# Softmax rows shifted inside four exponentials on ScalarE, in place of one subtraction on VectorE

## The chip, the cores and the metric

The kernel runs on one core of one Trainium2 chip. The metric is device microseconds (us) of one execution: the median of three runs is 2493.81 us (2492.76 to 2499.24). The engines are TensorE (PE, with its weight loads as PEld), VectorE (DVE), ScalarE (ACT), GpSimd (POOL) and SyncE (SP), which only starts transfers. Each engine works through its own list of instructions in order, and the lists meet in semaphores.

## The reference, cut to what matters

The program is one transformer layer over 32 sequences of 64 tokens, width 1024, in float32. The part that the change touches is the softmax of the attention (32 query heads, 8 key heads, head width 128):

```python
x = x + attn(einsum(x, cond_weights[condition]))       # q, k: RMS-normed by head
scores = einsum("bkgqd,bksd->bkgqs", q, k) / sqrt(128)
bias = where(rel > 0, -1e30, slopes * rel)             # ALiBi, causal, rel = key - query
attn = softmax(scores + bias, axis=-1)
out = (attn @ v) @ Wo.T
x = x + ffn(cond2(x))                                  # two linear layers with low-rank parts
```

## The kernel before, in words

The 2048 tokens go in four blocks of 512, each of four tiles of 128 tokens. Of each block the kernel works through units: keys and values of two key heads (`kv`), queries of one key head's four heads (`q`, eight of them), the output projection of a pair of key heads (`o`, four), and the two halves of the feed-forward layer (`f`). Every float32 operand is split into a high and a low part of the type fp32r, and a product is three matmuls (line 927). The high part is a copy on ScalarE (line 1122), the low part a subtraction on VectorE (line 1372). Of a chunk of weights both parts go into `ring`. The output projection takes seven products of half-size blocks instead of eight; its left factors are sums of quarters (`quads`), split into `lefts`. In block 0 the right factors are also summed on VectorE (`sums`). The projection is the same in both kernels.

The order of all work is written by one planner. A `q` step is one unit and one tile: four chunks of six matmuls of 512 columns, with a clock tick of the planner after each chunk (a quarter). What follows on the other engines is put in by delays in quarters (the table `AT`): squares and the mean (ACT, DVE), the power -0.5 (`rstd`, POOL), the scaling of the queries (`scale`, DVE line 1499, writes `qn`), their transposes (PE line 1076), their split (`qt_hi`, `qt_lo`), the scores (PE lines 1092 and 1093), the softmax, the transposes of the probabilities (PE line 1100), their split and the product with the values (PE line 1111), whose result ScalarE copies to `quads`. Work that falls between these by its delay, the split of a weight chunk above all, stands between them in the lists of the engines. There are 128 `q` steps in the program (8 units x 4 tiles x 4 blocks), and the softmax of step k runs beside the matmuls of step k+1.

The softmax of a step has 128 partitions x 256 columns, which are four row groups of 64 keys. Its instructions are `alibied` and `biased` (VectorE, line 1375: the two parts of the scores in PSUM and the ALiBi table are added into `score`), `peak` (line 1535: maximum of each row group), `shifted` (line 1541: the maximum subtracted, in place), `exp` (ScalarE, line 1270), `total`, `inverse` and `prob` (VectorE, lines 1546, 1551, 1556: sum, reciprocal, product). The planner adds the first four as one group at 5.5 quarters, `exp` at 6.3, the last three at 6.4 and the transposes of `prob` at 7.9.

## Time and profile before

| What | Value |
| --- | --- |
| Runs, median (lowest, highest) | 2493.81 us (2492.76, 2499.24) |
| Profiled execution, its own time | 2496.57 us |
| Its span, first to last instruction | 2494.8 us |
| Mean granted clock of TensorE | 0.987 of full speed |
| Share of the span busy: PE, DVE, ACT | 96%, 71%, 50% |

The profiled execution took 1.8 us more than its span, and 2.76 us more than the median of the runs. A busy time is a sum over one engine; it does not say that an engine sets the time. The chain that ended last is followed back from the last instruction, at each step to what released it. Where it passes through an instruction with a piece of 0.04 us, the next instruction on the same engine started before that one had ended, and only the part before that start is put down to it; what follows as "issue" belongs to the same stretch of the engine's list.

### The profile page before, as it was taken

The numbers are of one execution on the slowest core, as the hardware profiler recorded it, in microseconds if no ns is written. First come the engines' busy times: TensorE is split into PE (matmuls) and PEld (weight loads), VectorE is DVE, ScalarE is ACT, GpSimd is POOL, SyncE is SP. The second block draws the span as 40 slices with busy tenths as digits, with TensorE's granted clock in tenths as the row PEclk, the third lists the DMA queues.
The fourth block names the chain that finished last, engine by engine and source line by source line (L and its number), as shares of the span: only waits on it lengthen the run. The fifth ranks groups of instructions, "written<-read, shape, count | busy, mean of one in ns | idle before, by whom it ended". The sixth has DMA issues, their size and how long they took to land.

```text
span 2494.8 us, 32612 instructions
## 1 busy us (share of the span) xinstructions
PE 2407.1 (96%) x11676; PEld 1984.4 (80%) x11676; DVE 1777.3 (71%) x2894; ACT 1242.0 (50%) x2881; POOL 244.9 (10%) x272
## 2 busy tenths in 40 slices
PE   7999999999899999999899999999989999999988
PEld 5877778878788888888778888888868888888867
DVE  5547879796836878787854777777864686868772
ACT  3234646464624555555533555555633564646550
POOL 0101000000011101010011101010110101010110
PEclk8999999999999999999999999999999999999999
DMA  5355454543432242424233141424243242424240
GB/s 206 117 215 206 167 187 153 202 145 109 152 112 100 80 144 81 143 81 143 102 130 143 68 152 68 152 68 152 76 146 135 68 144 76 150 70 152 69 169 34
DMA packets 88435, 316.12 MB, mean 127 GB/s; under 512 B 12716, under 2 KB 13228, under 8 KB 87124
## 3 DMA queue, kind: packets, MB, share of 16 engines
q1 hardware_dynamic: 70292, 247.14, 28.9%
q10 hardware_dynamic: 10944, 37.54, 4.0%
q0 software_dynamic: 7040, 29.36, 3.2%
q8 instruction: 95, 1.56, 0.2%
q14 instruction: 64, 0.52, 0.1%
HBM read 282.54 MB, written 31.46 MB: 126 GB/s over the span
## 4 chain that ended last, share of the span: by engine, by line
PE 85%; DVE 10%; issue 3%; DMA 1%; ACT 1%; ACTq 0%; POOL 0%; POOLq 0%; DVEq 0%
PE main L927 72%; DVE ring L1372 3%; PE qt_bank L1076 3%; PE s_bank L1092 2%; PE pv_bank L1111 2%; PE s_bank L1093 2%; DVE score L1375 2%; PE pt_bank L1100 1%; DVE qn L1499 1%; PE pt_bank L927 1%; PE s_bank L927 1%; PE qt_bank L927 1%; DVE peak L1535 1%; DMA sums<-in_wo 1%; DVE pt_lo L1562 0%
## 5 line engine op out<-in xcount | busy, mean ns | idle before, releaser
L927 PE MATMUL main<-ring,act_hi 128*128 128x512 f32 x3584 | 1150.9, 402 | 0.0
L927 PEld LDWEIGHTS main<-ring,act_hi 128*128 128x128 f32 x3584 | 643.2, 189 | 111.5
L927 PE MATMUL main<-ring,act_lo 128*128 128x512 f32 x1792 | 702.9, 392 | 0.0
L927 PE MATMUL main<-ring,lefts 128*128 128x512 f32 x2688 | 636.8, 395 | 24.0 <-issue 23.9
L1372 DVE TENSOR_TENSOR ring<-raw,ring 128x1024 fp32r<-128x1024 f32 x448 | 556.9, 1244 | 80.0 <-ACT ring L1122 78.5
L927 PEld LDWEIGHTS main<-ring,lefts 128*128 128x128 f32 x2688 | 507.6, 190 | 131.9 <-issue 27.1
L1122 ACT ACTIVATE ring<-raw 128x1024 fp32r<-128x1024 f32 x448 | 473.0, 1057 | 239.4 <-PE main L927 234.4
L927 PEld LDWEIGHTS main<-ring,act_lo 128*128 128x128 f32 x1792 | 337.4, 188 | 74.8
L1695 POOL TENSOR_TENSOR rstd<-mean,half 128x4 f32<-128x4 f32 (+1 forms) x192 | 174.7, 910 | 1694.6 <-DVE mean L1482 1694.6
L1244 ACT ACTIVATE sq<-main 128x128 f32<-128x128 f32 x640 | 168.8, 277 | 66.1 <-PE main L927 63.7
L1375 DVE TENSOR_TENSOR acc<-main,acc 128x512 f32<-128x512 f32 x164 | 112.4, 686 | 98.2 <-PE main L927 98.1
L1270 ACT ACTIVATE prob<-score 128x256 f32<-128x256 f32 x128 | 53.5, 418 | 230.6 <-DVE score L1541 230.6
L1562 DVE TENSOR_TENSOR pt_lo<-pt_bank,pt_hi 64x256 fp32r<-64x256 f32 x256 | 107.9, 421 | 75.0 <-ACT pt_hi L1279 73.3
L1372 DVE TENSOR_TENSOR lefts<-quads,lefts 128x1024 fp32r<-128x1024 f32 x112 | 136.7, 1221 | 26.8 <-ACT lefts L1122 24.5
L1279 ACT ACTIVATE pt_hi<-pt_bank 64x256 fp32r<-64x256 f32 x256 | 97.1, 379 | 115.9 <-PE pt_bank L1100 111.3
L1122 ACT ACTIVATE qt_hi<-qt_bank 128x512 fp32r<-128x512 f32 x128 | 76.7, 599 | 129.8 <-PE qt_bank L1076 129.4
L1499 DVE TENSOR_TENSOR qn<-main,rstd 128x512 f32<-128x512 f32 (+1 forms) x192 | 114.6, 597 | 33.7 <-POOL rstd L1695 33.7
L1372 DVE TENSOR_TENSOR qt_lo<-qt_bank,qt_hi 128x512 fp32r<-128x512 f32 x128 | 88.2, 689 | 67.6 <-ACT qt_hi L1122 66.2
L1244 ACT ACTIVATION_READ_ACCUMULATOR sq<-main 128x1 f32 x640 | 132.6, 207 | 0.0
L1122 ACT ACTIVATE lefts<-quads 128x1024 fp32r<-128x1024 f32 x112 | 118.5, 1058 | 27.6 <-PE main L927 20.2
L1092 PE MATMUL s_bank<-k_t,qt_hi 128*128 128x128 f32 x512 | 114.7, 285 | 7.4 <-issue 7.4
L1076 PEld LDWEIGHTS qt_bank<-ident,qn 128*128 128x128 f32 x640 | 76.6, 141 | 53.1 <-DVE qn L1499 27.3
(142 smaller groups left out, 2445.1 us busy)
## 6 DMA issues: line engine op xcount, KB each, us to landing
raw<-in_wq SPq DMA_DIRECT2D x128, 512.0 KB, 4.2
raw<-t_scratch SPq DMA_DIRECT2D x128, 512.0 KB, 3.2
raw<-in_wo SPq DMA_DIRECT2D x96, 512.0 KB, 3.2
raw<-in_wkv SPq DMA_DIRECT2D x64, 512.0 KB, 3.4
sums<-in_wo ACTq DMA_DIRECT2D x32, 512.0 KB, 6.7
t_scratch<-sums ACTq DMA_DIRECT2D x32, 512.0 KB, 3.7
raw<-f_scratch SPq DMA_DIRECT2D x32, 512.0 KB, 4.4
acc<-in_x POOLq DMA_DIRECT2D x16, 512.0 KB, 3.6
```

Of the source, the lines that this page charges most:

```text
L927: mm = eng.matmul(bank, a, b, start=start and n == 0 and m == 0, stop=stop and n == len(terms) - 1 and m == 2, skip_group_check=further)
L1076: mm = eng.transpose(qt_bank[:, tile(h)], norm_tile(k)[:, tile(h)], ident[:, :])
L1092: eng.matmul(s_bank[:, a:a + 2 * SEQ], lh, keys, start=True, stop=False)
L1122: eng.activation(dst, src, ACT.Copy).then_inc(done[stage], 1)
L1244: act = eng.activation(sq[:, tile(h)], norm_bank(k)[:, tile(h)], ACT.Square, accum_out=ssum[:, h:h + 1])
L1270: eng.activation(prob[:, :], score[:, :], ACT.Exp).then_inc(done["exp"], 1)
L1279: act = eng.activation(pt_hi[rows_of(b), b, :], pt_bank[rows_of(b), 0:256], ACT.Copy)
L1372: eng.tensor_tensor(dst, src, f32(upper), ALU.subtract).then_inc(done[stage], 1)
L1375: eng.tensor_tensor(dst, a, b, ALU.add).then_inc(done[stage], 1)
L1499: eng.tensor_tensor(heads_of(norm_tile(k)[:, cols], heads), heads_of(norm_bank(k)[:, cols], heads), along(rstd[:, 0:heads], heads), ALU.mu ...
L1562: rest = eng.tensor_tensor(pt_lo[rows_of(b), b, :], pt_bank[rows_of(b), 0:256], f32(pt_hi[rows_of(b), b, :]), ALU.subtract)
L1695: eng.tensor_tensor(rstd[:, 0:heads], mean[:, 0:heads], half[:, 0:heads], ALU.pow).then_inc(done[stage], 1)
```

## The change: minimum of the negated scores as the bias of four exponentials

The scores are now kept negated: the table `alibi` is negated on the host, `alibied` is table minus the first part of the scores, `biased` subtracts the second part. The maximum becomes a minimum of the negated rows. `shifted` is gone. The exponential takes -1 times the negated score plus the minimum of its row group. That minimum is a column of 128 values and differs from row group to row group, so the one instruction over 256 columns becomes four over 64 columns. The last of the four raises the semaphore that `total` waits for; the first waits for `peak`.

```diff
             self.queries_left = "score", (k,)
 
         def softmax():
-            for stage in ("alibied", "biased", "peak", "shifted"):
+            for stage in ("alibied", "biased", "peak"):
                 self.add(stage, k)
...
                 elif stage == "exp":
                     k, = key
-                    w.wait_ge("shifted", k)
+                    w.wait_ge("peak", k)
                     if order.number["prob_t", key] > 1:
                         w.wait_ge("prob_t", order.stages_of["prob_t"][order.number["prob_t", key] - 2][0])
                     else:
                         w.wait_ge("ones")
-                    eng.activation(prob[:, :], score[:, :], ACT.Exp).then_inc(done["exp"], 1)
+                    for r in range(4):
+                        cols = slice(r * SEQ, (r + 1) * SEQ)
+                        act = eng.activation(prob[:, cols], score[:, cols], ACT.Exp, bias=peak[:, r:r + 1], scale=-1.0)
+                    act.then_inc(done["exp"], 1)
...
                         table = alibi[:, 2 * g:2 * g + 2, :].rearrange("p h (o n) -> p h o n", o=1)
-                        add(rows, parts[:, :, :, 0, :], table.broadcast_to([P, 2, BPT, SEQ]), stage)
+                        eng.tensor_tensor(rows, table.broadcast_to([P, 2, BPT, SEQ]), parts[:, :, :, 0, :],
+                                          ALU.subtract).then_inc(done[stage], 1)
                     else:
                         w.wait_ge("alibied", k)
-                        add(rows, parts[:, :, :, 1, :], rows, stage)
+                        eng.tensor_tensor(rows, rows, parts[:, :, :, 1, :], ALU.subtract).then_inc(done[stage], 1)
                 elif stage == "peak":
                     k, = key
                     w.wait_ge("biased", k)
                     eng.tensor_reduce(peak[:, :], score[:, :].rearrange("p (r n) -> p r n", n=SEQ), AXIS.X,
-                                      ALU.max).then_inc(done[stage], 1)
-                elif stage == "shifted":
-                    k, = key
-                    w.wait_ge("peak", k)
-                    by_row = score[:, :].rearrange("p (r n) -> p r n", n=SEQ)
-                    eng.tensor_tensor(by_row, by_row, peak[:, :].rearrange("p (r o) -> p r o", o=1).broadcast_to([P, 4, SEQ]),
-                                      ALU.subtract).then_inc(done[stage], 1)
+                                      ALU.min).then_inc(done[stage], 1)
...
-    return table.reshape(HEADS // 2, 2, SEQ, SEQ).transpose(1, 2, 0, 3).reshape(P, HEADS // 2, SEQ)
+    return -table.reshape(HEADS // 2, 2, SEQ, SEQ).transpose(1, 2, 0, 3).reshape(P, HEADS // 2, SEQ)
```

On VectorE, in the third `q` step of block 1 (`ring` is the split of a weight chunk, `qn` the scaling of the next step's queries), there stands before:

```order
L1375 TENSOR_TENSOR score<-s_bank,alibi 128x256 [waits s_score]
L1375 TENSOR_TENSOR score<-s_bank,score 128x256 [waits s_alibied]
L1535 TENSOR_REDUCE peak<-score 128x4 [waits s_biased]
L1541 TENSOR_TENSOR score<-score,peak 128x256 [waits s_peak]
L1372 TENSOR_TENSOR ring<-raw_65,ring 128x1024 [waits s_w_hi]
L1499 TENSOR_TENSOR qn_72<-main,rstd 128x512 [waits s_query_t,s_rstd]
L1546 TENSOR_REDUCE total<-prob 128x4 [waits s_exp]
```

and now:

```order
L1532 TENSOR_TENSOR score<-alibi,s_bank 128x256 [waits s_score]
L1536 TENSOR_TENSOR score<-score,s_bank 128x256 [waits s_alibied]
L1540 TENSOR_REDUCE peak<-score 128x4 [waits s_biased]
L1375 TENSOR_TENSOR ring<-raw_65,ring 128x1024 [waits s_w_hi]
L1502 TENSOR_TENSOR qn_72<-main,rstd 128x512 [waits s_query_t,s_rstd]
L1545 TENSOR_REDUCE total<-prob 128x4 [waits s_exp]
```

The row of line 1541 is gone and nothing else has moved: the split of the weights, the scaling and `total` follow in the same order, one place earlier.

On ScalarE, at the same step (`quads` is the copy of the previous step's attention output, `ring` the high part of a weight chunk, `qt_hi` that of the transposed queries), there stands before:

```order
L1122 ACTIVATE ring<-raw_65 128x1024 [waits s_raw1]
L1270 ACTIVATE prob<-score 128x256 [waits s_shifted]
L1122 ACTIVATE quads<-pv_bank 128x2x4x64 [waits s_pv]
L1122 ACTIVATE ring<-raw_66 128x1024 [waits s_raw2]
L1122 ACTIVATE qt_hi<-qt_bank 128x4x2x64 [waits s_score,s_query_t]
```

and now:

```order
L1122 ACTIVATE ring<-raw_65 128x1024 [waits s_raw1]
L1272 ACTIVATE prob<-score,peak 128x64 [waits s_peak]
L1272 ACTIVATE prob<-score,peak 128x64 x3
L1122 ACTIVATE quads<-pv_bank 128x2x4x64 [waits s_pv]
L1122 ACTIVATE ring<-raw_66 128x1024 [waits s_raw2]
L1122 ACTIVATE qt_hi<-qt_bank 128x4x2x64 [waits s_score,s_query_t]
```

One exponential has become four at the same place, the first with a wait for `peak` in place of `shifted`; the copies behind them keep their order.

## Rows read from the trace of the kernel before

**Rows 1.** The page: busy us (share of the span) and instructions.

```profile
PE 2407.1 (96%) x11676; PEld 1984.4 (80%) x11676; DVE 1777.3 (71%) x2894; ACT 1242.0 (50%) x2881; POOL 244.9 (10%) x272
```

**Rows 2.** Waits: who waited <- for what: us in total, times, longest us.

```profile
ACT prob L1270 <- DVE score L1541: 230.6, 127, 5.6
...
PEld qt_bank L1076 <- DVE qn L1499: 27.3, 41, 3.6
...
PE main L927 <- issue: 23.9, 6, 5.8
...
PEld pt_bank L1100 <- DVE prob L1556: 2.9, 7, 0.5
```

**Rows 3.** Two stretches: length, busy PE PEld DVE ACT POOL, PEclk, DMA.

```profile
780.00:1204.00 424.00, 423.17 (x2067) 349.74 (x2067) 324.50 (x566) 235.67 (x593) 39.32 (x43) 1.00 0.31 107
1204.00:1245.00 41.00, 34.44 (x161) 27.70 (x160) 37.38 (x57) 25.93 (x52) 2.02 (x2) 0.94 0.37 128
```

**Rows 4.** Timeline of a step: start us, us, engine, line.

```profile
811.78 1.01 POOL L1695 TENSOR_TENSOR rstd<-mean,half 128x4 f32<-128x4 f32 x1 [6.76 <-DVE mean L1482]
...
812.67 0.42 DVE L1535 TENSOR_REDUCE peak<-score 128x4 f32<-128x256 f32 x1
...
813.12 0.42 DVE L1541 TENSOR_TENSOR score<-score,peak 128x256 f32<-128x256 f32 x1
...
813.46 1.22 DVE L1372 TENSOR_TENSOR ring<-raw,ring 128x1024 fp32r<-128x1024 f32 x1
...
813.58 0.42 ACT L1270 ACTIVATE prob<-score 128x256 f32<-128x256 f32 x1 [1.12 <-DVE score L1541]
813.90 0.59 ACT L1122 ACTIVATE quads<-pv_bank 128x512 f32<-128x512 f32 x1
...
814.60 0.68 DVE L1499 TENSOR_TENSOR qn<-main,rstd 128x512 f32<-128x512 f32 x1
...
814.38 0.61 PE L927 MATMUL main<-ring,act_hi 128*128 128x512 f32 x2
814.83 0.39 PE L927 MATMUL main<-ring,act_lo 128*128 128x512 f32 x1
815.34 0.66 PE L1076 MATMUL qt_bank<-ident,qn 128*128 128x128 f32 x4
```

**Rows 5.** Chain that ended last: start us, us, what.

```profile
202.24 0.04 DVE score L1541
...
1208.41 0.04 DVE score L1541
...
1216.82 0.04 DVE score L1541
...
1225.65 0.42 DVE score L1541
...
2382.93 0.42 DVE score L1541
```

**Rows 6.** Groups by line and shape: count, busy us, mean ns, idle before.

```profile
L1541 DVE TENSOR_TENSOR score<-score,peak 128x256 f32<-128x256 f32 x128 | 54.4, 425 | 4.4
...
L1270 ACT ACTIVATE prob<-score 128x256 f32<-128x256 f32 x128 | 53.5, 418 | 230.6 <-DVE score L1541 230.6
```

**Rows 7.** Line 1407, PSUM as its second operand: ns min/median/max.

```profile
L1407 DVE TENSOR_TENSOR qn<-kept,main x2: 673/676/680, 21.5 to 23.5; 40x512 f32<-40x512 f32 x2
```

**Rows 8.** ScalarE instructions back to back.

```profile
9.81 0.70 ACT L1152 ACTIVATE pt_hi<-prob 128x256 fp32r<-128x256 f32 x2
...
11.04 0.29 ACT L1122 ACTIVATE qt_hi<-prob 128x128 fp32r<-128x128 f32 x1
...
1212.61 0.77 ACT L1279 ACTIVATE pt_hi<-pt_bank 64x256 fp32r<-64x256 f32 x2 [1.02 <-PE pt_bank L1100]
```

**Rows 9.** Timeline of a step: probabilities done, loaded by PE.

```profile
1047.69 0.42 DVE L1556 TENSOR_TENSOR prob<-prob,inv 128x256 f32<-128x256 f32 x1
...
1048.94 0.37 PEld L1100 LDWEIGHTS pt_bank<-ident,prob 128*128 128x128 f32 x2
```

## The prediction

> **What bounds the kernel now.** I read the busy shares first, then the waits, two stretches by their busy times, the chain that ended last, and at last single steps in order of time. TensorE is busy 96% of the span, VectorE 71%, ScalarE 50% [rows 1]. Between 780 and 1204 us TensorE's records fill 423.17 of 424 us and VectorE's 324.50; from 1204 to 1245 us TensorE's fill 34.44 of 41 and VectorE's 37.38 [rows 3]. So TensorE bounds the kernel in most places, and at the end of a block VectorE does. What VectorE costs elsewhere must be looked for in short waits: the transposes of the queries wait for the scaling `qn` 41 times, 27.3 us in all, and at the end of a block the projection waits up to 5.8 us [rows 2]. ScalarE has waited for the subtraction 127 times before its exponential, 230.6 us in all [rows 2]; that is cover in front of the exponential, and shows that ScalarE is the early one there.
>
> **The subtraction goes.** Each of the 128 takes 425 ns, 54.4 us in all [rows 6]. In the step at 813 us the maximum starts at 812.67, the subtraction at 813.12, the split of a weight chunk at 813.46 [rows 4]. The last started 0.34 us after the instruction before it; behind the maximum it would start at 813.01. So 0.45 us of VectorE's list goes per step, 57.6 us over 128. It is worth time only where the subtraction is on the path. It stands in the chain that ended last 44 times, from 202.24 to 2382.93 us [rows 5]. I sort the 44 by what follows.
>
> *Short waits, 26 times.* Behind the subtraction stand a split of 1.22 us and the scaling, and TensorE waits for the latter. In the step shown, two products take from 814.38 to 814.83, thus 0.225 us each. The transposes start 0.51 us after the product at 814.83, which is 0.28 us late [rows 4]. With the scaling 0.45 us earlier (from 814.60 to 814.15) nothing is left of that. Nor is another releaser just behind: GpSimd's `rstd` ended at 812.79 [rows 4]. 26 x 0.28 = 7.3 us.
>
> *Block 0, six times.* There the sums of the right factors stand in the same list, and VectorE works without a pause from the subtraction to the instruction that TensorE waits for. Each gives its whole 0.45 us: 2.7 us.
>
> *Ends of blocks, three in each of four.* In block 1 these are at 1208.41, 1216.82 and 1225.65 us [rows 5]. VectorE is busy 37.38 of those 41 us [rows 3], and the projection behind them waits up to 5.8 us [rows 2]. A shorter list moves the end of that wait by all that it is shortened: 12 x 0.45 = 5.4 us.
>
> The other 84 subtractions are not in the chain. TensorE's products hide them, and I count them at nothing. If that cover were gone they would be worth 84 x 0.45 = 38 us.
>
> **Four exponentials for one.** The present one takes 418 ns [rows 6]. The trace has no exponential of 64 columns and none whose bias is a column. Nearest from below: copies from SBUF of 256 columns, two in 0.70 us, so thus 0.40 us each and 0.30 apart, an overlap of 0.10; one of 128 columns takes 0.29 us [rows 8]. On this line 64 columns take 0.24 us and start 0.14 apart: four take 3 x 0.14 + 0.24 = 0.66 us. From above: the two copies of 256 columns and 64 partitions from PSUM take 0.77 us and don't overlap, 0.385 each [rows 8]; four such take 1.54 us. I take 0.66, since the copies from SBUF are the nearer rows, and keep 1.54 for the range. The exponentials start 0.45 us earlier than now (behind the maximum), so they end 0.45 - (0.66 - 0.42) = 0.21 us earlier than now, or 0.67 us later by the upper bound. What is queued behind them is the copy of the attention output (at 813.90 in the step shown) [rows 4] and the high part of the next weight chunk; what waits for them is `total`. In the step at 1046 us `total` follows the exponential directly, the normalised rows are done at 1047.69 + 0.42 = 1048.11 and TensorE loads them at 1048.94 [rows 9]: 0.83 us to spare, more than 0.67. TensorE waited for `prob` only 7 times, 2.9 us in all [rows 2]. So in most steps even the upper bound costs nothing. At the ends of blocks it does: there ScalarE's copies feed VectorE's list, and 0.67 us later would eat the 0.45 us of each subtraction. By the upper bound the 12 give nothing, or lose 12 x 0.22 = 2.6 us more if all of it shows.
>
> The Trainium skill (ScalarE: Activation LUTs, What ACT_TABLE_LOAD costs) has a rule that speaks against this change: an ACTIVATE costs a fixed 186 ns and 0.833 ns a column, a bias that is a column adds about 93 ns, and neighbours overlap by about 93 ns. The present trace agrees on the fixed part and the overlap (0.40 us for 256 columns, 0.30 apart) and is silent on the bias. By that page four take 3 x 0.24 + 0.33 = 1.05 us; the sum would then lose about 0.1 us at each of the twelve places, and the time would come out some 1.2 us higher.
>
> **Edits at nothing.** Adding becomes subtracting and maximum becomes minimum on the same shapes. The PSUM operand becomes the second one; a 512-column instruction of that kind takes 676 ns [rows 7], one with PSUM first 0.68 us [rows 4]. The bounds are -0.01 and +0.01 us, 256 times on VectorE, of which 88 in the chain: under 1 us either way. The negated table is made on the host; its transfer is the same. No transfer is moved.
>
> **The sum.** 7.3 + 2.7 + 5.4 = 15.4 us. The profiled execution took 2496.57 us and would take 2481.2; the median of the runs is 2.76 us lower, so I predict 2493.81 - 15.4 = 2478.4 us, 0.6% less.
>
> **The rivals.**
> 1. *The short waits come back or were never the bound (no change).* The chain credits VectorE wherever it released TensorE last, even if by a hair, and the weight split before the scaling needs a high part from ScalarE, which now works longer. If the 26 short waits stay and the ends of blocks give nothing, 2.7 us are left: 2491 us. For it: in [rows 3] TensorE's records fill the long stretch but for 0.83 us, so there is little to see. Against it: the 0.51 us between two starts in [rows 4] is a gap in the starts themselves.
> 2. *ScalarE becomes the late one (slower).* The mechanism is one: the exponentials end so late that `prob` reaches the transposes late in ordinary steps. The place is line 1100, the point is 0.83 + 0.45 + 0.42 = 1.70 us for the four, 0.425 each without overlap [rows 9]. For it: an exponential takes 0.418 now, and reading a bias column is unseen. Against it: 256 columns become 64. At 0.5 us each the four take 2.0, 0.3 us beyond the point; if half of the 128 steps have no more slack than the one shown, 64 x 0.3 = 19 us are added, the ends of blocks give nothing, and it ends at 2493.8 - 10.0 + 19 = 2503 us.
> 3. *More than the sum (faster still).* The granted clock at the end of block 1 is 0.94 against 1.00 in the long stretch [rows 3]: TensorE runs part of it at 1.2 GHz, after its long wait. 0.06 of 41 us is 2.5 us; if the shorter waits spare it that, four blocks give 10 us more, 2468 us. Against it: a wait of 5.8 us less 1.35 is still a long one.
>
> **How the numbers follow.** The forecast has 0.70, within 2473 to 2486 by the bounds of the exponentials (upper bound: 2493.8 - 10.0 + 2.6 = 2486.4) and by the count of 44. Rival 1 has 0.16, rival 2 0.07, rival 3 0.05, 0.02 is left for what I don't see. The range 2471 to 2489 us takes in the forecast's own and the near parts of rivals 1 and 3. A difference of 0.3% (7.5 us, so below 2486.3 or above 2501.3) is about what a measurement can tell from none. Faster: forecast 0.70, rival 3 0.05, and a quarter of rival 1 (0.04), in which the ends of blocks still give their 5.4 us: 0.79. Same: the rest of rival 1 (0.12) and 0.01: 0.13. Slower: rival 2 (0.07) and 0.01: 0.08.
>
> **What would show it.** In the profile after: the waits of TensorE's loads for `qn` at line 1502 down from 27.3 us to under 15 and from 41 times to some 15; the starts of product and transposes at the step shown 0.23 us apart; line 1272 with 512 exponentials of 0.24 us `total` 0.45 us earlier or close to it; VectorE's busy time down by about 54 us; the waits at the ends of blocks ending earlier by 1.3 us each relative to the first of their three steps. I am wrong if the short waits keep their count, if an exponential of 64 columns takes over 0.4 us, or if loads at the transposes of `prob` wait more than 7 times.

## The result and the profile after

The kernel after takes 2481.80 us, median of four runs (2481.04 to 2483.35). Four runs of the kernel before on the same chip, three of them those of the first table, have a median of 2496.52 us (2492.76 to 2501.97). The ratio is 0.994, with a 95% interval of 0.9918 to 0.9962: 14.7 us less. The profiled execution has a span of 2481.6 us against 2494.8, 13.2 us less. The forecast of 2478.4 us is 3.4 us off, inside its range. Of these, 2.7 us lie in its starting point: it counted from 2493.81 us, and with a fourth run the kernel before stands at 2496.52. The sum of 15.4 us stands against 14.7 in the runs and 13.2 in the profiles.

From the page of the kernel after (busy us, share of the span, instructions; then the chain that ended last; then the group of the exponentials):

```profile
PE 2399.1 (97%) x11676; PEld 1986.9 (80%) x11676; DVE 1725.9 (70%) x2766; ACT 1322.0 (53%) x3265; POOL 244.9 (10%) x272
...
PE 89%; DVE 6%; issue 2%; DMA 2%; ACT 1%; ACTq 0%; POOL 0%; POOLq 0%; DVEq 0%
...
L1272 ACT ACTIVATE prob<-score,peak 128x64 f32<-128x64 f32 x512 | 136.7, 338 | 171.0 <-DVE peak L1540 171.0
```

Against [rows 1] VectorE is busy 51.4 us less and ScalarE 80.0 us more. In the chain that ended last VectorE has 6% instead of 10, TensorE 89 instead of 85; before, that line was:

```profile
PE 85%; DVE 10%; issue 3%; DMA 1%; ACT 1%; ACTq 0%; POOL 0%; POOLq 0%; DVEq 0%
```

The last row of the page after answers to both of [rows 6]: the 54.4 us of subtractions are gone, the exponentials take 136.7 us instead of 53.5, and ScalarE still stands idle for 171.0 us in front of them (230.6 before). The idle time that was named as cover has paid for the longer exponential, and most of it is left.

Next the waits of the kernel after (engine, line, waited for: us in total, times, longest us), which answer to [rows 2]:

```profile
DVE total L1545 <- ACT prob L1272: 44.2, 86, 0.8
...
PE main L927 <- issue: 24.3, 7, 6.0
...
PEld qt_bank L1076 <- DVE qn L1502: 6.3, 7, 3.1
...
PEld pt_bank L1100 <- DVE prob L1555: 1.2, 5, 0.4
```

The loads' waits for the scaling `qn` fell from 27.3 us and 41 times to 6.3 and 7. A new wait has come, of VectorE for the exponentials, 86 times and 44.2 us. What `total` hands on is not late by it: the transposes of `prob` wait less than before (1.2 us instead of 2.9). The long waits of the projection at the ends of blocks are as long as they were (24.3 us instead of 23.9).

The same step as in [rows 4], in the timeline of the kernel after (start us, us, what, in brackets the idle time before and its releaser):

```profile
809.58 0.42 DVE L1540 TENSOR_REDUCE peak<-score 128x4 f32<-128x256 f32 x1
...
810.03 1.06 ACT L1272 ACTIVATE prob<-score,peak 128x64 f32<-128x64 f32 x4 [0.68 <-DVE peak L1540]
...
811.04 0.68 DVE L1502 TENSOR_TENSOR qn<-main,rstd 128x512 f32<-128x512 f32 x1
...
811.65 0.41 DVE L1545 TENSOR_REDUCE total<-prob 128x4 f32<-128x256 f32 x1
...
811.75 0.40 PE L927 MATMUL main<-ring,act_lo 128*128 128x512 f32 x1
811.99 0.60 PE L1076 MATMUL qt_bank<-ident,qn 128*128 128x128 f32 x4
...
812.30 0.43 DVE L1555 TENSOR_TENSOR prob<-prob,inv 128x256 f32<-128x256 f32 x1
...
813.59 0.37 PEld L1100 LDWEIGHTS pt_bank<-ident,prob 128*128 128x128 f32 x2
```

From the start of the maximum to the start of the scaling it is 1.46 us, where it was 1.93 [rows 4]. The transposes start 0.24 us after the product before them instead of 0.51, so TensorE does not stop. The exponentials take 1.06 us instead of 0.42 and end 1.51 us after the maximum's start, where the one ended 1.33 us after it: 0.18 later, not 0.21 earlier as forecast. The normalised rows are done at 812.73 and loaded at 813.59, so 0.86 us are still to spare.

**Where the 13.2 us of the two profiles came from.** The point at which TensorE starts again after its long wait at the end of a block divides the time. In the kernel before these points are 662.42, 1240.85, 1819.92 and 2398.12 us. In the timeline of the kernel after:

```profile
659.55 6.78 PE L927 MATMUL main<-ring,lefts 128*128 128x512 f32 x21 [5.96 <-issue]
...
1234.44 2.05 PE L927 MATMUL main<-ring,lefts 128*128 128x512 f32 x4 [5.81 <-issue]
...
1810.12 1.19 PE L927 MATMUL main<-ring,lefts 128*128 128x512 f32 x2 [5.83 <-issue]
...
2384.85 1.62 PE L927 MATMUL main<-ring,lefts 128*128 128x512 f32 x3 [5.83 <-issue]
```

Up to the end of block 0 it is 2.9 us less; blocks 1 to 3 take 1725.30 us instead of 1735.70, 10.4 less; what follows them is the same within 0.1. In block 1 (578.43 us before, 574.89 after) both kernels make the same 2792 matmuls in the same order, so the distance from one start to the next can be compared pair by pair. The difference of 3.54 us stands in a few places (us between two starts):

```
place in block 1                                        before    after     gives
7 steps: product -> first transpose of the queries      0.51      0.23      7 x 0.27 = 1.92
the same steps: first -> second transpose               0.165     0.109     7 x 0.06 = 0.40
end of block, step at 1217.9: product -> transposes     1.136     0.226     0.91
end of block, transposes of prob at 1227.96             0.478     0.340     0.14
two products of the projection right behind the start   0.764     0.569     0.20
```

Together 3.57; all other places together take 0.03 back. So a short wait was worth 0.33 us and not 0.28: the second transpose came late too, since its weight load had started late with the first one's. And the end of a block gives its share at the transposes of the queries, 0.91 us, and at those of `prob`; the long wait behind them only starts and ends earlier.

**Block 0, compared in the same way.** Here a second profile of the kernel after helps (it comes again among the experiments; its block 0 ends at 654.85 us, 7.6 us earlier than before). Fourteen subtractions of this block stood in the chain. The stops of TensorE behind them, fourteen too, at transposes of the queries and of `prob` from 203.3 to 649.8 us, give the same in both profiles (each with its second transpose), and what differs lies elsewhere:

```
places in block 0 (us that the kernel after gives)      first profile    second profile
ten stops at transposes of the queries                  4.56             4.59
four stops at transposes of `prob`                      0.90             0.91
all else                                                -2.6             +2.1
```

That is 5.46 and 5.50 us, where the prediction counted 5.45. A large part of the rest stands at two starts of the scores, 336.29 and 463.50 us in the kernel before. They wait for `qt_lo`, which stands on VectorE behind additions of `sums`, and one of these waits for a transfer. At the second place, before and in the second profile of the kernel after (the line of the first profile, with 2.25 us, is shown among the experiments):

```profile
460.32 1.23 DVE L1615 TENSOR_TENSOR sums<-sums,sums 128x1024 f32<-128x1024 f32 x1 [0.39 <-DMA sums<-in_wo]
```

```profile
455.14 1.22 DVE L1614 TENSOR_TENSOR sums<-sums,sums 128x1024 f32<-128x1024 f32 x1 [1.14 <-DMA sums<-in_wo]
```

```
                                                  before    after, first    after, second
336.29: VectorE idle for the transfer             2.00      1.24            0.38
        last product -> scores                    2.62      1.88            0.99
463.50: VectorE idle for the transfer             0.39      2.25            1.14
        last product -> scores                    1.01      2.89            1.77
```

The stops grow and shrink with the waits for the transfers, to 0.02 us. In the first profile the granted clock also stood at 1.2 GHz for 3.4 us from 335.6 us on; at this place it stood at 2.4 GHz in the other two. In blocks 1 to 3 all transposes of queries and of `prob` together give 10.15 and 10.21 us, so that the places named by the forecast give 15.6 and 15.7 us in the two profiles, with 15.4 forecast.

### The profile page after: what moved, and what is told of

It reads as the page before. It is cut to its first block, busy times and chain, and to the rows that moved or that the text cites. A ratio compares the mean times of both kernels' runs of the same rounds, so it can differ in the third digit from the quotient of the medians.

```text
span 2481.6 us, 32868 instructions
## 1 busy us (share of the span) xinstructions
PE 2399.1 (97%) x11676; PEld 1986.9 (80%) x11676; DVE 1725.9 (70%) x2766; ACT 1322.0 (53%) x3265; POOL 244.9 (10%) x272
## 4 chain that ended last, share of the span: by engine, by line
PE 89%; DVE 6%; issue 2%; DMA 2%; ACT 1%; ACTq 0%; POOL 0%; POOLq 0%; DVEq 0%
PE main L927 75%; PE pv_bank L1111 3%; PE qt_bank L1076 3%; PE s_bank L1092 2%; DVE ring L1375 2%; PE s_bank L1093 2%; PE pt_bank L1100 1%; DMA sums<-in_wo 1%; PE pt_bank L927 1%; PE s_bank L927 1%; PE qt_bank L927 1%; DVE lefts L1375 0%; DVE pt_lo L1561 0%; DVE acc L1378 0%; PE qt_bank L1015 0%
## 5 line engine op out<-in xcount | busy, mean ns | idle before, releaser
L927 PE MATMUL main<-ring,lefts 128*128 128x512 f32 x2688 | 636.3, 395 | 24.4 <-issue 24.3
L1272 ACT ACTIVATE prob<-score,peak 128x64 f32<-128x64 f32 x512 | 136.7, 338 | 171.0 <-DVE peak L1540 171.0
L1093 PE MATMUL s_bank<-k_t,qt_lo 128*128 128x64 f32 x512 | 117.2, 245 | 0.0
```

The source lines that it names most:

```text
L927: mm = eng.matmul(bank, a, b, start=start and n == 0 and m == 0, stop=stop and n == len(terms) - 1 and m == 2, skip_group_check=further)
L1093: mm = eng.matmul(s_bank[:, a:a + SEQ], ll, keys[:, 0:SEQ], start=False, stop=True)
L1272: act = eng.activation(prob[:, cols], score[:, cols], ACT.Exp, bias=peak[:, r:r + 1], scale=-1.0)
```

## The experiments

All comparisons are with the kernel before on the same chip. The first four kernels shared 18 runs of it (2496.71 us), the next four 15 (2497.34), the last four 11 (2495.13). The diffs are against the kernel after unless said otherwise. A stop in the starts means that a transpose starts more than 0.23 us after the product before it; its length is what goes beyond that, and stops of under 0.1 us are not counted.

### Only the 44 steps whose subtraction stood in the chain, and only the other 84

```diff
+            if not fused(n):            # n-th softmax; 44 numbers, or the other 84
+                self.add("shifted", k)
...
-                    w.wait_ge("peak", k)
+                    w.wait_ge("peak" if k in order.fused else "shifted", k)
...
+                    if k in order.fused:
+                        for r in range(4): ...   # as in the kernel after
+                    else:
+                        act = eng.activation(prob[:, :], score[:, :], ACT.Exp, scale=-1.0)
```

> The subtraction is left out (with four exponentials) only in the 44 steps in which it stood in the chain that ended last; the other 84 steps keep a subtraction and one exponential. Theory A (the subtraction is worth something only where it stood in that chain): the whole gain of the change, 11 to 16 us below before, ratio 0.9935 to 0.9955. Rival B (VectorE's load as a whole sets the time, each subtraction worth the same): 44/128 of the change's 13 to 15 us, so 4 to 5 us, ratio about 0.998.

> The reverse: the subtraction is left out only in the 84 steps in which it did not stand in the chain. Theory A: no gain, within 2 us of before, ratio 0.999 to 1.001; the waits of the transposes for the scaled queries stay at about 41 times and 27 us. Rival B: 84/128 of the gain, 9 us, ratio about 0.996.

The 44 alone: 2479.97 us, ratio 0.9933 (0.992 to 0.9946). The other 84 alone: 2495.88 us, ratio 1.0 (0.999 to 1.0009). The waits of the two, first the 44, then the 84:

```profile
PEld qt_bank L1087 <- DVE qn L1516: 6.9, 12, 3.1
```

```profile
PEld qt_bank L1091 <- DVE qn L1520: 25.4, 37, 3.6
```

The whole gain is in the 44 (16.7 us, a little more than the 11 to 16 expected); on the other 84 steps the change is worth nothing within 2.5 us either way, with all of its exponentials. Blocks 1 to 3 take 1725.4 us with the 44, as in the kernel after.

### The four exponentials without the gain, and the gain with one exponential

The first is against the kernel before: the subtraction stays, and the four exponentials add the maximum back.

```diff
-                    eng.activation(prob[:, :], score[:, :], ACT.Exp).then_inc(done["exp"], 1)
+                    for r in range(4):
+                        cols = slice(r * SEQ, (r + 1) * SEQ)
+                        act = eng.activation(prob[:, cols], score[:, cols], ACT.Exp, bias=peak[:, r:r + 1])
+                    act.then_inc(done["exp"], 1)
```

The second computes the minimum and doesn't use it:

```diff
-                    for r in range(4):
-                        cols = slice(r * SEQ, (r + 1) * SEQ)
-                        act = eng.activation(prob[:, cols], score[:, cols], ACT.Exp, bias=peak[:, r:r + 1], scale=-1.0)
-                    act.then_inc(done["exp"], 1)
+                    eng.activation(prob[:, :], score[:, :], ACT.Exp, scale=-1.0).then_inc(done["exp"], 1)
```

> The kernel before with its subtraction, and four exponentials of 64 columns with the maximum as bias in place of the one (the values are those of a softmax without its shift). It measures the four alone, without the 0.45 us that the change gives them: they end 0.64 us later than before. Theory A (ScalarE has slack): 0.83 us of slack at the transposes hides them in ordinary steps, and only the ends of blocks pay, at most 12 x 0.64 = 7.7 us; I expect 0 to 5 us above before, ratio 1.000 to 1.002. Rival C (ScalarE is next to be late): 20 us or more above before, and more than 30 waits for the normalised rows at the transposes.

> The changed kernel with one exponential over 256 columns and no bias, so that the shift by the maximum is left out of the computation: the gain of the removed subtraction alone. Theory A: 0 to 3 us below the changed kernel, 13 to 18 us below before, ratio 0.993 to 0.995. Rival C: the four exponentials eat a large part of the gain, so at least 6 us below the changed kernel, ratio 0.991 or less.

Four exponentials behind the subtraction: 2504.87 us, ratio 1.0029 (1.0018 to 1.0041), 8.2 us more than before. That is above what I had expected of it. Its waits:

```profile
DVE total L1549 <- ACT prob L1272: 43.5, 86, 0.5
PEld qt_bank L1076 <- DVE qn L1502: 30.3, 40, 4.0
...
PEld pt_bank L1100 <- DVE prob L1559: 4.1, 7, 0.7
```

The loads wait for `qn` as often as before (40 times), but longer: the stop before the transposes of the queries is 0.41 us where it was 0.28, and at the four ends of blocks the transposes of `prob` stop for 0.39 where it was 0.08. Blocks 1 to 3 take 1739.60 us, 3.9 more than before; the 21 short stops make 2.7 of it and the three at `prob` 0.9. The rest, 5.7 us, lies in block 0 (its end at 668.16 instead of 662.42), 1.6 of it at the two starts of scores that follow the transfers (VectorE's idle times there are 0.4 and 1.1 us longer than before), so not all of it is the price of the exponentials. How a longer exponential lengthens the wait for the *queries* is seen on VectorE, from the step before to the step that stops (timeline of this kernel):

```profile
811.26 0.69 DVE L1502 TENSOR_TENSOR qn<-main,rstd 128x512 f32<-128x512 f32 x1
812.47 0.42 DVE L1549 TENSOR_REDUCE total<-prob 128x4 f32<-128x256 f32 x1 [0.53 <-ACT prob L1272]
...
820.28 0.68 DVE L1502 TENSOR_TENSOR qn<-main,rstd 128x512 f32<-128x512 f32 x1
...
821.02 0.66 PE L1076 MATMUL qt_bank<-ident,qn 128*128 128x128 f32 x4 [0.25 <-DVE qn L1502]
```

From one scaling to the next it is 9.02 us; in the kernel before the two start 8.88 us apart (the second is the one at 814.60 in [rows 4]). In the first of the two steps no split stands in front of `total`, so VectorE waits 0.53 us for the exponentials. It makes up for most of that with the short idle times behind, and 0.14 us is left and reaches the scaling of the next step: the 0.13 by which each stop has grown. So the price is paid one step later, in another instruction than the one that waits.

One exponential and no subtraction: 2478.38 us, ratio 0.992 (0.9908 to 0.9933). That is 18.3 us less than before, against 14.7 for the kernel after, so a little more than theory A allowed and less than rival C asked for; the intervals of the two ratios overlap. Its blocks 1 to 3 take 1725.1 us in the profile, those of the kernel after 1725.3. At the fourteen places of block 0 it gives 5.52 us against before, the kernel after 5.46 and 5.50. So at these places the other three exponentials cost nothing that the profiles show; where the few us between the medians come from stays open. The price of four exponentials depends on the room in VectorE's list: beside the subtraction it is 3.9 us in blocks 1 to 3, without the subtraction 0.2.

### The subtraction twice

Against the kernel before; the maximum is subtracted a second time.

```diff
-            for stage in ("alibied", "biased", "peak", "shifted"):
+            for stage in ("alibied", "biased", "peak", "shifted", "again"):
                 self.add(stage, k)
```

> The kernel before with the subtraction done twice in all 128 steps, so that the softmax is shifted by twice the maximum. Theory A (VectorE's list matters by position): each of the 44 places on the path costs its 0.45 us, 19.8 us, and places that had under 0.45 us of slack join them, so 20 to 30 us above before, ratio 1.008 to 1.012. Rival B (load as a whole): the mirror image of the change, 13 to 16 us above before, ratio 1.006.

2524.21 us, ratio 1.0108 (1.0093 to 1.0124), 26.9 us more than before, within theory A. As its waits have it:

```profile
PEld qt_bank L1076 <- DVE qn L1499: 54.4, 57, 4.4
```

In its starts 67 stops stand before transposes of queries, 41.1 us, where before had 47 with 18.3: the short ones of an ordinary step are 0.73 instead of 0.28, which is the whole 0.45 of the added instruction, and new ones of 0.26 to 0.28 have come in steps where before had none. So the same 0.45 us is worth 14.7 us taken away and 26.9 us added: on the one side there was 0.28 to win at most in an ordinary step, on the other there is no such end, and steps that had cover have used it up.

### Eight and sixteen exponentials

Of 32 and of 16 columns, with the same biases.

```diff
-                    for r in range(4):
-                        cols = slice(r * SEQ, (r + 1) * SEQ)
+                    for i in range(8):          # or 16
+                        r, cols = i * 4 // 8, slice(i * 256 // 8, (i + 1) * 256 // 8)
```

> The changed kernel with eight exponentials of 32 columns a step. From the rows of the changed kernel (64 columns: 335 ns, started 240 ns apart) eight take 7 x 0.21 + 0.31 = 1.8 us against 1.06, just beyond the point of 1.70 us that the prediction gave. Theory A: VectorE waits for them in its list before the sum, so short waits come back; 8 to 20 us above the changed kernel, ratio to before 0.997 to 1.002. Rival D (no such point near, ScalarE has 47% of its time free): within 3 us of the changed kernel, ratio 0.994 to 0.995.

> The same with sixteen exponentials of 16 columns: 15 x 0.20 + 0.29 = 3.3 us a step, 2.2 us more than four. Theory A: far beyond the point, each ordinary step pays 1.6 us less what else hides it, 60 to 200 us above before, ratio 1.024 to 1.08. Rival D: the extra 290 us of ScalarE stay hidden but for the ends of blocks, under 20 us above before, ratio below 1.008.

Eight: 2501.54 us, ratio 1.0016 (1.0007 to 1.0026), 4.2 us more than before, so some 19 us over the kernel after. Sixteen: 2652.05 us, ratio 1.0618 (1.0602 to 1.0634), 155 us more than before. Both are within theory A; rival D falls. The same ordinary step with eight, and its waits:

```profile
808.68 1.80 ACT L1272 ACTIVATE prob<-score,peak 128x32 f32<-128x32 f32 x8 [0.68 <-DVE peak L1540]
```

```profile
DVE total L1545 <- ACT prob L1272: 111.8, 94, 1.4
PEld qt_bank L1076 <- DVE qn L1502: 20.7, 35, 3.6
PEld pt_bank L1100 <- DVE prob L1555: 13.2, 28, 1.7
```

And with sixteen:

```profile
864.76 3.29 ACT L1272 ACTIVATE prob<-score,peak 128x16 f32<-128x16 f32 x16 [2.11 <-DVE peak L1540]
```

```profile
PEld pt_bank L1100 <- DVE prob L1555: 153.8, 126, 3.1
```

At 1.80 us, 0.10 beyond the point of 1.70 that rival 2 had worked out, TensorE stops at `prob` 9 times in its starts: six times in block 0, and at the ends of blocks 1 to 3 with 1.36 to 1.39 us each, 6.9 us together. In ordinary steps of blocks 1 to 3 it does not stop yet, but the loads wait for `prob` in 28 steps (5 in the kernel after), and in every eighth step of these blocks the first transpose is 0.01 us late. So in these steps the point lies at 1.80 us, 0.10 beyond where it was put. The short waits for `qn` are back, with 0.18 to 0.23 us each; in blocks 1 to 3 the queries' transposes give up 6.6 us against the kernel after, those of `prob` 4.6. At 3.29 us TensorE stops at `prob` in 125 of 128 steps, 120.6 us. Before the point is reached, the same delay goes through VectorE's list and comes out at the queries. Rival 2 had the wrong first victim.

### The row sums by ScalarE's accumulator

```diff
-            for stage in ("total", "inverse", "prob"):
+            for stage in ("inverse", "prob"):
...
-                        act = eng.activation(prob[:, cols], score[:, cols], ACT.Exp, bias=peak[:, r:r + 1], scale=-1.0)
+                        act = eng.activation(prob[:, cols], score[:, cols], ACT.Exp, bias=peak[:, r:r + 1], scale=-1.0,
+                                             accum_out=total[:, r:r + 1])
```

> The changed kernel, in which each of the four exponentials also gives the sum of its rows, so that VectorE's sum (0.41 us, 128 times) is gone too. Theory A: the sum stands 8 times in the chain of the changed kernel, 8 x 0.44 = 3.5 us, less what the reading of four accumulators adds on ScalarE (0.09 us each by the squares' rows, 0.35 us a step, which is under the 0.44 us saved before the reciprocal): 0 to 4 us below the changed kernel, ratio to before 0.992 to 0.994. Rival C (ScalarE is next to be late): 2 us or more above the changed kernel, ratio 0.995 or more.

2481.99 us, ratio 0.9942 (0.9928 to 0.9955): as the kernel after (0.994), at the edge of theory A and short of rival C. The readings of the accumulator (duration in ns least, median, most; first and last start), the first exponential and the last reading of one step, and the wait behind them:

```profile
L1272 ACT ACTIVATION_READ_ACCUMULATOR prob<-score,peak x512: 185/187/213, 201.6 to 2369.9; 128x1 f32 x171
...
808.08 0.35 ACT L1272 ACTIVATE prob<-score,peak 128x64 f32<-128x64 f32 x1 [0.67 <-DVE peak L1541]
...
809.33 0.19 ACT L1272 ACTIVATION_READ_ACCUMULATOR prob<-score,peak 128x1 f32 x1
```

```profile
DVE inv L1546 <- ACT prob L1272: 78.3, 90, 1.4
```

From the first start to the last end the step takes 1.44 us instead of 1.07 (medians of the 128 steps of both kernels): the four readings lie partly under the exponentials and add 0.37 us, a little less than the 0.44 us by which `inverse` used to follow `total`. VectorE has another 128 instructions fewer, and waits for the exponentials 78.3 us instead of 44.2: 34 of the some 54 us that it saves (128 sums of 0.42) it spends waiting. The other 20 us buy no time either: after the first change the short waits are gone, and `total` stands in the chain of the kernel after only 8 times.

### The kernel after once more, and the sums of the right factors later

In the profile of the kernel after block 0 had given only 2.9 us, and VectorE waited there for transfers of the sums, with 2.25 us at one place:

```profile
459.84 1.22 DVE L1614 TENSOR_TENSOR sums<-sums,sums 128x1024 f32<-128x1024 f32 x1 [2.25 <-DMA sums<-in_wo]
```

So the same kernel was profiled again, to see how much of that belongs to one execution, and another was made in which the additions of the right factors' quarters in block 0 come 1.5 quarters later behind their loads:

```diff
             for i, stage in enumerate(("t1", "t2", "t3", "t4")):
-                self.at(start + apart * c, 6 + 0.8 * i, lambda c=c, stage=stage: self.add(stage, pair, c))
-            self.at(start + apart * c, 9.7, lambda c=c: stores(c))
+                self.at(start + apart * c, 7.5 + 0.8 * i, lambda c=c, stage=stage: self.add(stage, pair, c))
+            self.at(start + apart * c, 11.2, lambda c=c: stores(c))
```

> The changed kernel once more, on the same chip as the next three. Time within 3 us of its first runs (2481.8 us), ratio 0.993 to 0.995. Open is block 0, which gave 2.8 us of the 5.45 that the prediction counts there. Theory A: the transfers of the right factors' sums land earlier or later from run to run; the end of the long wait of block 0 (659.6 us in its first profile) moves by a microsecond or more, the lengths of blocks 1 to 3 stay within 0.5 us in their sum. Rival E: block 0 loses by the change itself; it repeats within 0.5 us.

> The changed kernel with the sums of the right factors (block 0 only) and their stores 1.5 quarters, about 2 us, later in the order. Theory A (VectorE waited there for transfers that land late): VectorE's waits for the transfers of the sums fall from 5.6 us to under 2 us, block 0 is 1 to 3 us shorter, ratio to before 0.992 to 0.9935. Rival F (the sums' own 1.2 us each in the list cost, wherever they stand): no change against the changed kernel, within 1 us.

Again: 2481.18 us, ratio 0.9945 (0.9932 to 0.9958), with a span of 2477.3 us. The end of block 0 in this profile, and in that of the later sums:

```profile
654.85 1.62 PE L927 MATMUL main<-ring,lefts 128*128 128x512 f32 x3 [5.97 <-issue]
...
2380.67 0.77 PE L927 MATMUL main<-ring,lefts 128*128 128x512 f32 x1 [5.84 <-issue]
```

```profile
649.38 1.19 PE L927 MATMUL main<-ring,lefts 128*128 128x512 f32 x2 [5.97 <-issue]
...
2374.14 1.19 PE L927 MATMUL main<-ring,lefts 128*128 128x512 f32 x2 [5.81 <-issue]
```

One kernel has its end of block 0 at 659.55 and at 654.85 us in two executions, and blocks 1 to 3 at 1725.30 and 1725.82: theory A, with no sign of rival E. What block 0 gives can't be read from the ends of one pair of profiles to better than some 5 us; pair by pair, as above, it can. The kernel with later sums takes 2472.32 us, ratio 0.9904 (0.9889 to 0.9918), 8.9 us below the kernel after in the same set, and these intervals don't overlap. I had expected less of it (a block 0 shorter by 1 to 3 us). Its blocks 1 to 3 take 1724.76 us, so all is in block 0. The waits of TensorE there, in the first profile of the kernel after and in this one:

```profile
PE s_bank L1092 <- issue: 8.2, 5, 2.5
...
PE qt_bank L927 <- DVE k_t L1375: 5.7, 1, 5.7
```

```profile
PE s_bank L1092 <- issue: 3.0, 2, 2.2
...
PE qt_bank L927 <- DVE k_t L1375: 2.6, 1, 2.6
```

That is 8.3 us of the 10.2 between the two ends of block 0; from the second profile of the kernel after it is 5.5 us between the ends. Additions that wait in VectorE's list for a transfer hold up the splits behind them, and TensorE the scores and the first product of the next stage. The waits for transfers are not all of it. In the kernel after the scores at 375.12 and 502.31 us start 1.36 and 1.35 us after the product before them, with no wait for a transfer in front: at the second place two additions, at 499.26 and 500.40 us, stand before the split `qt_lo` at 501.53. With the later sums both starts are 0.23 us apart. So the additions' own 1.2 us in the list cost too, by the place where they stand, and rival F was wrong only in "wherever". Other stops came in their stead, of 0.72 to 0.74 us before five transposes of queries, so this placing is not the last word.

### The addition of the seventh product behind the sums at the end of a block

The long wait at the end of a block ends with the split of `lefts`. In front of the sums that it needs stand two additions of the seventh product, 1.22 us each. This edit puts them later in the last pair of key heads.

```diff
-        self.later(1.5, lambda: self.add("v7_add", k, tp))
+        last = self.units[self.steps[k][0]][2] == KV_HEADS // 2 - 1
+        self.later(5.6 if last else 1.5, lambda: self.add("v7_add", k, tp))
```

> The changed kernel, in which at the end of a block (last pair only) the two additions of 1.2 us at line 1599 stand behind the sum of quarters and the split that TensorE waits 6 us for, in place of before them. Theory A (VectorE's list sets the end of that wait): 2.28 us shorter wait in each of four blocks, 9 us below the changed kernel, ratio to before 0.990 to 0.992. Rival G (another engine or a transfer sets it): within 2 us of the changed kernel.

> The changed kernel with both: the sums later and the two additions behind. Theory A: the two gains add up, 10 to 12 us below the changed kernel, ratio to before 0.989 to 0.991. If either theory falls, only the other's part.

No gain: 2482.81 us, ratio 0.9947 (0.9934 to 0.996), where the kernel after of the same set had 0.9945. The end of block 1 in its timeline:

```profile
1223.68 1.23 DVE L1376 TENSOR_TENSOR ring<-raw,ring 128x1024 fp32r<-128x1024 f32 x1 [1.01 <-ACT ring L1123]
...
1225.54 1.22 DVE L1576 TENSOR_TENSOR quads<-quads 128x1024 f32<-128x1024 f32 x1
1226.67 1.22 DVE L1600 TENSOR_TENSOR acc<-acc,kept 128x1024 f32<-128x1024 f32 x1
...
1230.68 1.22 DVE L1376 TENSOR_TENSOR lefts<-quads,lefts 128x1024 fp32r<-128x1024 f32 x1
...
1232.11 2.47 PE L928 MATMUL main<-ring,lefts 128*128 128x512 f32 x5 [6.42 <-issue]
```

The edit did not do what it was meant to. In the kernel after both additions stand in front of the two sums (at 1222.86 and 1226.02, the sums at 1229.01 and 1231.88); here one has moved into the stretch between the first sum, at 1225.54, and the split at 1230.68, and only the other, at 1231.81, stands behind it. And the room made in front is idle time: VectorE now waits for the high part of a weight chunk (1.01 us at 1223.68), and ScalarE in its turn stood 0.30 us for TensorE before it wrote the next one, at 1224.43. TensorE's wait got longer, 6.42 us instead of 5.81, and the blocks no shorter: 1 to 3 take 1727.7 us, where the two profiles of the kernel after had 1725.3 and 1725.8. That speaks for VectorE's list as what ends the wait, since an addition put into it made it longer, and not for rival G; what a real removal would give was not run. With both edits together 2474.19 us, ratio 0.9914 (0.9901 to 0.9927): the gain of the later sums, and nothing more. The version with the later sums alone has the lowest time of all that were run.

## Why the prediction was right, point by point

- **Faster, by the sum's size: right.** 15.4 us forecast, 14.7 measured, interval of the ratio 0.9918 to 0.9962. The ratio was 0.9945 in a second set. That the sum fits so closely is in part luck: two of its terms are off in opposite directions, as follows. The lower end of the forecast's own range, 2473 us, has no sum behind it.
- **"I sort the 44 by what follows"; the other 84 at nothing: right, and shown.** The 44 alone give 0.9933, the 84 alone 1.0.
- **Short waits, 26 x 0.28 us: right in number, a little small in size.** The listed waits for `qn` fell to 7; all seven in block 1 are gone. Each gave 0.33 us, since the second transpose no longer comes late either; over the 21 of blocks 1 to 3 that is 1.1 us more than counted.
- **Ends of blocks, 3 x 0.45 us each: a little too large, and not in its place.** In block 1 the end gave 0.91 at the transposes of the queries and 0.14 at those of `prob`, 1.05 of 1.35 us. Three such are 0.9 us less than counted. I had put it at the long wait, which kept its length. Over blocks 1 to 3 both terms were to give 21 x 0.28 + 9 x 0.45 = 9.9 us; the profiles show 10.4 (9.9 with the second profile of the kernel after).
- **Block 0, six whole subtractions and five short waits: right in sum.** With its share of the ends of blocks it was to give 5.45 us, and the fourteen places gave 5.46 and 5.50. One by one they give 0.13 to 0.93 us, so "Each gives its whole 0.45 us" holds as an average and not for each. The ends of block 0 say 2.9 and 7.6 us, because VectorE's waits for transfers differ from execution to execution by more than that; the prediction has no such term.
- **Four exponentials in 0.66 us: mis-sized.** They take 1.06. This is the one cost of the prediction that was clearly wrong. The fixed time that I read off copies in [rows 8] came out too small for an instruction with a bias column, and so did the distance between starts, 0.24 us and not 0.14. The estimate by the rule of the Trainium skill (ScalarE: Activation LUTs, What ACT_TABLE_LOAD costs), 1.05 us, agrees with this trace. The error cost the forecast nearly nothing, because ScalarE was idle there and VectorE had the room; the run with the subtraction beside the four exponentials shows the cost without that room. That they would end 0.21 us earlier than now was therefore wrong too: counted from the maximum they end 0.18 later in the step shown. The 0.1 us that the prediction took off each end of a block by that rule is not worked out there; between one exponential and four, blocks 1 to 3 show 0.2 us over nine such places.
- **`prob` to spare 0.83 us, point of rival 2 at 1.70 us: right in place, incomplete.** At 1.06 us no ordinary step of blocks 1 to 3 stops at `prob`, at 1.80 every eighth just begins to, at 3.29 nearly all do. But at 1.80 VectorE's wait for the exponential had already brought back the waits for `qn`, and I had left this wait out: I named `total` as what waits, and not what is queued behind `total`.
- **`total` 0.45 us earlier: right in the step shown, not in all.** There it starts 2.07 us after the maximum, against 2.53 before: there the maximum started at 812.67 [rows 4] and `total` at 815.20. In the steps where nothing stands in front of it, it now waits for the exponentials, 86 times and up to 0.8 us.
- **Rival 1 (nothing to win) and rival 3 (the clock):** against rival 1 stands the whole result. For rival 3 there is nothing: the granted clock in the 41 us around the end of block 1 is 0.93 after and 0.94 before, as the window of after shows.

```profile
1198.00:1239.00 41.00, 35.19 (x165) 28.57 (x164) 36.63 (x55) 27.94 (x62) 2.02 (x2) 0.93 0.37 128
```

This row answers to the second of [rows 3] (after the window's length: busy us and instructions of PE, PEld, DVE, ACT, POOL; then granted clock, DMA share, GB/s). VectorE is busy 36.63 of the last 41 us still: the end of the block is its place as before.

## What to carry to other kernels

An instruction taken from an engine that doesn't bound the kernel is worth what the bounding engine's stops behind it are long, stop by stop: sort the places where it stands in the chain that ended last, cap each with the gap in the starts of the bounding engine, and count the rest at nothing. A stage whose waits hang on transfers has to be compared place by place, not by its end: in block 0 the ends said 2.9 and 7.6 us where the places said 5.5 both times. The same 0.45 us per step was worth 14.7 us taken away and 26.9 us added. Work that is moved to an idle engine is free only as long as nobody waits for it in order; look at what is queued behind the waiting instruction, not only at what it hands on. With eight exponentials most of the loss in ordinary steps came out there.

## What the runs showed of the hardware that was not expected

These are readings of this kernel's traces, on one core.

- An exponential with a bias column takes 335 ns for 64 columns, 307 for 32 and 293 for 16 (medians), and neighbours start 0.24, 0.21 and 0.20 us apart (four in 1.06, eight in 1.80, sixteen in 3.29 us). With a quarter of the columns only 42 ns are saved per instruction of 335.

```profile
L1272 ACT ACTIVATE prob<-score,peak x1024: 304/307/333, 202.2 to 2389.9; 128x32 f32<-128x32 f32 x171
```

```profile
L1272 ACT ACTIVATE prob<-score,peak x2048: 290/293/318, 201.6 to 2541.1; 128x16 f32<-128x16 f32 x187
```

- A reading of ScalarE's accumulator after an exponential is recorded with 187 ns, but four of them lengthen a step's exponentials by 0.37 us only, 0.09 us each, because they overlap their neighbours.
- A late weight load costs twice: after a stop of 0.27 us before the first transpose, the second starts 0.165 us behind it and not 0.109; after one of 0.73 us (the subtraction twice) it is 0.165 too.
- One kernel, with one order of instructions, had its block 0 end at 659.55 and 654.85 us in two executions, while the other three blocks together took 1725.30 and 1725.82.
